# First attention layer: two-operand forms in place of copies and tensor_scalar on VectorE

## The reference

```
q, k, v = x @ Wq + bq, x @ Wk + bk, x @ Wv + bv          # 8 heads of 32
time_diff = edge_time - node_time[dst]
time_features = stack([sign(time_diff), log1p(abs(time_diff) / 3600)])
scores = sum(q[dst] * k[src]) * 32**-0.5 + time_features @ Wt + bt
alpha = softmax(scores, over all edges)                   # per head
out = segment_sum(alpha * v[src], dst) @ Wo + bo
```

## Time and profile before

| | us |
|---|---|
| median of three runs | 9245.88 |
| span of the profiled execution, first to last instruction | 9211.3 |
| first attention layer (loops of all engines) | about 1209 to 3996, 2787 |
| VectorE busy in that stretch | 1941.89 |
| GpSimd busy in that stretch | 1721.17 |
| TensorE busy in that stretch | 1501.30 |
| ScalarE busy in that stretch | 911.31 |

### The profile page before, as it was taken

One profiled execution on the slowest core, in us unless ns is written; L12 is line 12 of the kernel. 1 busy time (PEld: TensorE's weight loads), 2 busy tenths in 40 slices (PEclk: granted clock), 3 DMA queues, 4 the chain that ended last, 5 costly groups with the idle time before them and its releaser, 6 DMA issues. The chain is left out here.

```text
span 9211.3 us, 125505 instructions
## 1 busy us (share of the span) xinstructions
PE 5882.9 (64%) x27440; PEld 4000.9 (43%) x27441; DVE 5920.1 (64%) x16481; ACT 2399.3 (26%) x6580; POOL 5832.9 (63%) x6228
## 2 busy tenths in 40 slices
PE   2121145555555555559999996999999996545544
PEld 0010023333333333337777764566666664333333
DVE  4010056767777676658999986999999996222224
ACT  0000023333333333323333332444444442000000
POOL 5777756666666666647777762666666665666663
PEclk6555567777667767679999997999999998776776
DMA  1000033333333333323333352444444444333334
GB/s 67 1 8 10 10 88 90 91 90 89 92 88 92 87 88 87 90 57 84 88 90 87 85 83 55 120 126 123 126 123 126 123 125 95 90 91 91 90 90 53
DMA packets 406142, 779.80 MB, mean 85 GB/s; under 512 B 195939, under 2 KB 225357, under 8 KB 405197
## 3 DMA queue, kind: packets, MB, share of 16 engines
q0 software_dynamic: 279488, 712.60, 30.3%
q1 hardware_dynamic: 126348, 64.59, 2.5%
HBM read 736.75 MB, written 40.07 MB: 84 GB/s over the span
## 5 line engine op out<-in xcount | busy, mean ns | idle before, releaser
L982 POOL DMA_INDIRECT gat<-kv,rec_sb_d x896 | 861.6, 962 | 816.5 <-DVE big L1320 521.9
L1884 POOL DMA_INDIRECT gat<-y,rec_sb_s x892 | 1027.1, 1151 | 424.0 <-issue 285.4
L2153 POOL DMA_INDIRECT gat<-x,rec_sb_d x892 | 845.4, 948 | 477.7 <-issue 255.6
L1421 POOL DMA_INDIRECT gat<-kv,rec_sb_s x900 | 861.7, 957 | 415.2 <-issue 313.8
L2168 PE MATMUL ps<-gat,oh 128*128 128x256 f32 x1760 | 644.8, 535 | 676.2 <-DVE acc L2188 235.4
L1616 DVE TENSOR_REDUCE small<-ps 128x2 f32<-128x1024 f32 x884 | 1042.4, 1217 | 5.3 <-PE ps L1484 4.0
L434 POOL DMA_INDIRECT rec_d<-small x784 | 811.7, 1035 | 341.9 <-issue 263.2
L1925 PE MATMUL ps<-big,oh 128*128 128x256 f32 x3520 | 907.7, 390 | 0.0
L489 POOL DMA_INDIRECT rec_s<-wts,rows x770 | 758.7, 985 | 234.7 <-issue 234.7
L1028 PE MATMUL ps<-qz,work 128*128 x1792 | 770.2, 605 | 143.2 <-issue 125.7
L2168 PEld LDWEIGHTS ps<-gat,oh 128*128 128x128 f32 x1760 | 461.0, 273 | 859.7 <-issue 558.2
(11 more groups left out here) (278 smaller groups left out, 12710.2 us busy)
## 6 DMA issues: line engine op xcount, KB each, us to landing
gat<-kv,rec_sb_s POOLq DMA_INDIRECT x900
gat<-kv,rec_sb_d POOLq DMA_INDIRECT x896
rec_sb_s<-rec_s SPq DMA_DIRECT2D x448, 32.0 KB
gat<-y,rec_sb_s POOLq DMA_INDIRECT x892
gat<-x,rec_sb_d POOLq DMA_INDIRECT x892
rec_d<-small POOLq DMA_INDIRECT x784
rec_s<-wts,rows POOLq DMA_INDIRECT x770
rec_s<-gat SPq DMA_DIRECT2D x4, 1808.0 KB, 17.0
```

Source lines behind the costliest of these rows:

```text
L982: e.indirect_dma_start(out=gat[:, m.u, q, :], out_offset=None, in_=table, in_offset=bass.IndirectOffsetOnAxis(ap=r_sb[:, m.u, q, 0:1].bitc ...
L1421: e.indirect_dma_start(out=gat[:, m.u, q, :], out_offset=None, in_=table, in_offset=bass.IndirectOffsetOnAxis(ap=r_sb[:, m.u, q, 0:1].bitc ...
L1884: e.indirect_dma_start(out=rows_y[m.u][:, q, :], out_offset=None, in_=y1, in_offset=bass.IndirectOffsetOnAxis(ap=r_sb[:, m.u, q, 0:1].bitc ...
L2153: e.indirect_dma_start(out=gat[:, m.u, q, 0:D], out_offset=None, in_=x3, in_offset=bass.IndirectOffsetOnAxis(ap=r_sb[:, m.u, q, 0:1].bitca ...
```

## The change

Every VectorE instruction of the loop that had one tensor operand in SBUF as a copy or a `tensor_scalar` is written with two tensor operands in SBUF. A copy becomes `max(x, x)`. The one-hots become two instructions of 128 by 256 instead of four of 128 by 128, comparing two broadcast views; `oh` is given with the second. They stand where the first two stood; where the third and the fourth stood, nothing is left. The sign takes a column of -1 (`minus_one`) in place of the immediate.

```diff
+            minus_one = col(576, 4)
+            def two_one_hots(e, m, q):
+                if q == 0:
+                    have_record(e, m)
+                    e.wait_ge(s["sum"], m.done(U))
+                ins = V.tensor_tensor(oh[:, m.u, q:q + 2, :], bcast(iota[:, :], 1, [P, 2, P]),
+                                      bcast(r_sb[:, m.u, q:q + 2, 1], 2, [P, 2, P]), ALU.is_equal)
+                if q + 2 == Q:
+                    ins.then_inc(s["oh"], 1)
+
+            def move(to, of):
+                return V.tensor_tensor(to, of, of, ALU.max)
 # times_1
-                k = c(V.tensor_scalar(sg, td, 0.0, -1.0, ALU.is_gt, ALU.add))
+                k = c(V.scalar_tensor_tensor(sg, td, 0.0, minus_one, ALU.is_gt, ALU.add))
 # score_timed
                 k = c(V.transpose(mq32_t, mq32))
                 ja = bucket(e, a)
-                one_hot(e, nxt, 0)
+                two_one_hots(e, nxt, 0)
                 c.wait(k)
                 k = c(V.tensor_reduce(by_block[:, 0:1], mq32_t, AX.X, ALU.max))
-                one_hot(e, nxt, 1)
+                two_one_hots(e, nxt, 2)
                 c.wait(k)
                 for n in range(1, 4):
-                    k = c(V.tensor_copy(by_block[0:32, n:n + 1], by_block[32 * n:32 * n + 32, 0:1]))
-                one_hot(e, nxt, 2)
+                    k = c(move(by_block[0:32, n:n + 1], by_block[32 * n:32 * n + 32, 0:1]))
                 c.wait(k)
                 k = c(V.tensor_reduce(mr, by_block[0:32, :], AX.X, ALU.max))
-                one_hot(e, nxt, 3)
                 c.wait(k)
-                k = c(V.tensor_copy(top32[0:32, :], mr.to_broadcast([32, 32])))
+                k = c(move(top32[0:32, :], mr.to_broadcast([32, 32])))
...
                 for n in range(1, 4):
-                    k = c(V.tensor_copy(top32_t[32 * n:32 * n + 32, 0:H], top32_t[0:32, 0:H]))
+                    k = c(move(top32_t[32 * n:32 * n + 32, 0:H], top32_t[0:32, 0:H]))
...
-                V.tensor_scalar(mj, mn, 1.0, None, ALU.mult).then_inc(s["f"], 1)
+                move(mj, mn).then_inc(s["f"], 1)
```

More of the change, by code:

```diff
@@ L1338, in dve @@
                     c(V.memset(mq32, 0.0))
+                    c(V.memset(minus_one, -1.0))
                     c.wait()
@@ L1342, in dve @@
                 for m in range(AHEAD - 1):
+                    if timed:
+                        two_one_hots(e, Macro(0, m), 0)
+                        two_one_hots(e, Macro(0, m), 2)
+                        continue
                     for q in range(Q):
```

## The result

| | median us (runs) | lowest to highest |
|---|---|---|
| before | 9231.44 (7) | 9214.21 to 9260.86 |
| after | 9194.72 (7) | 9157.15 to 9222.61 |

The ratio is 0.995, with 0.993 to 0.9971 as its 95% interval: 37 us gained, where 84 were forecast. The profiled execution of after is the slowest of its seven (9222.61 us), so its span, 9.5 us longer than that of before, must not be read as a loss. It also shows that only 1.8 us lie around a span, not the 34.6 us of the forecast: that difference was the spread between runs.

A forecast was written before the change was run, and what follows sets the result against it. VectorE was taken to set the pace, with GpSimd 2.4 us per turn from doing so. 3 x 0.3 + 0.6 = 1.5 us per pass over 56 passes, 84 us, took 9246 to about 9160; range 8970 to 9300, for faster alone 9085 to 9225.

The forecast's parts named there:

- Faster, 9160: Whole kernel: median falls from 9246 to about 9160 us; faster was given 0.55, this forecast itself 0.38.
- The sum of 84 us: Changed layer: 0.3 us in each of three turns plus 0.6 in the long one, over 56 passes.
- The change can't touch the loop's jump: VectorE's loop: the 3.45 us ahead of L1313 once a pass of four turns would stay.
- Relief of the small forms, 0.3 us in each of three turns: VectorE's copies at L1258: two-operand forms stall less, saving 0.3 us in each of a pass's three calm turns.
- rival 2: VectorE's dependent instructions stall in GpSimd's burst whatever their form, so no change: 9246, less or more 40 us; chance 0.22.
- Calm turn unchanged: VectorE's turns other than the long one: shorter one-hots and unfilled gaps change them by -0.3 to +0.6 us, taken as 0.
- The stall of L1209 stays near 65 us: VectorE's L1209 keeps its form, so its idle time, 65.3 us in 168 turns, was to remain.
- A long turn gives back little, since ScalarE is late by itself: Once a pass, ScalarE's L1127 starts late without VectorE's doing, so the 15.29 us turn gives back only 0.6 us.
- Rival 3: GpSimd loses its rest, bringing a second long turn in some passes, 5.0 us each: slower, 9300 us; chance 0.18.
- GpSimd has 2.4 us per turn to spare: GpSimd waits 2.4 us per turn for L1320, so relief of VectorE can bring at most 537 us.
- Rival 1: The lock between VectorE's copies or tensor_scalars and GpSimd explains all: rewritten lines' stalls go, 312 us, 8970; chance 0.22.
- The signs named: Changed layer: 84 us shorter, one turn in four over 14 us, L1127 late, L1209 idle near 65 us; later stages unchanged.

The follow-up runs named there:

- experiment 1: Changed kernel with copies, sign and running maximum in their old forms, so only the one-hots are changed: 9196.24 us, 0.9947.
- experiment 2: Changed kernel with four tensor_scalar one-hots back at their old places, so only moves, sign and running maximum are changed: 9227.92 us, 0.9998.
- experiment 5: Kernel before and changed kernel, each with GpSimd's scatters of this layer left out: 8871.99 us (0.9619) and 8635.76 us (0.9355).
- experiment 4: Changed kernel with four two-operand one-hots of 128x128 at the old four places instead of two wide ones: 9160.87 us, 0.992.
- experiment 3: Changed kernel with three more semaphore increments per turn on VectorE, for which nobody waits: 9205.0 us, 0.9964.
- experiment 7: Changed kernel with GpSimd waiting, between gathers and scatters, until ScalarE has evacuated the transposes: 9000.29 us, 0.9763.
- k1: Kernel before, with scatters waiting for ScalarE's evacuation and the next turn's record copied ahead of them, on a third chip: 8456.67 us, 1.0035.
- k4: Kernel of experiment 1, with scatters waiting for ScalarE's evacuation and the next record copied ahead of them, on a third chip: 8483.6 us, 1.0067.
- k2: Changed kernel, with scatters waiting for ScalarE's evacuation and the next turn's record copied ahead of them, on a third chip: 8449.15 us, 1.0032.

## Why the prediction was right and wrong

- *Faster, 9160.* Measured 9194.72: the direction holds, and the time lies within the range. That is luck. The sum of 84 us was right in nothing but its order of size, for its terms were not what moved the time.
- *"The change can't touch the loop's jump."* This is the step that failed most. It removed nearly all of it: 149.5 to 19.1 us ahead of the multiply, 174 us over the layer. The row was in front of me, as was the row of queue 14 on the page, and I took 3.45 us once a pass for a property of jumps. A change that rewrites a loop must be asked what it does to the fetching of its code. That the one-hots' rewriting removed it, experiments 1, 2 and 5 show, and experiment 4 by its 169.2 us as well; that the count of instructions is the reason isn't shown, and experiment 3 speaks against it.
- *Relief of the small forms, 0.3 us in each of three turns.* Experiment 2 gives 0 (within 0.2% of the time). The stalls ahead of the moves stayed, as rival 2 said: 126.5 and 128.7 us for 121.1.
- *Calm turn unchanged.* It went from 9.68 to 9.27 us (1803.12 to 1812.39 in after), 0.1 us outside the bounds of -0.3 to +0.6.
- *The stall of L1209 stays near 65 us.* It fell to 21.8; those of L1244 and of the last move rose, from 16.8 to 36.4 and from 17.2 to 36.5. A stall falls on whatever VectorE has just then; its place is no property of the line. That was wrong, and with it the reasoning line by line from the earlier trace rows.
- *A long turn gives back little, since ScalarE is late by itself.* Right, and it is the core of the case. The long turns stayed, and grew by 0.5 us. ScalarE's release hangs on GpSimd's burst (experiments 5 and 7). But ScalarE is late by TensorE's signal and not by itself, and the earlier trace rows, which were to show the same wait elsewhere, are waits for TensorE's matmuls as far as k1's trace tells.
- *Rival 3, a second long turn.* Its mechanism came: 1.29 turns over 14 us per pass became 1.76. It comes with the jump's 3.45 us and not with the small forms: ScalarE starts over 5 us late in 40 to 47 of some 200 turns with the jump paid (before and experiment 4) and in 33 of 191 in experiment 2, but in 82 to 93 of some 193 without it (after, experiments 1 and 3). That the 3.45 us had served as GpSimd's rest once a pass is my reading; no run tests it. Its sum was too dark because some 174 us stood on the other side, not 84.
- *GpSimd has 2.4 us per turn to spare.* True as a mean, and misleading: in the pair read it waits 4.50 us for L1331 in one turn and not at all in the next, and the pair takes 24.96 us, as two mean turns of before do.
- *Rival 1, the lock alone, 8970.* Its 312 us are near only to the 236 us that the change brings without the scatters, and for another reason. With the scatters the stalls are there for two-operand forms as well.
- *The signs named.* One turn in four was to be over 14 us; it was 86 in 195. The sign of rival 2, the moves idling as the copies did, came. That of rival 3 came by half: more long turns, but GpSimd's wait ahead of the gathers fell, from 402.9 to 379.9 us. The stages behind the layer didn't keep their lengths, by the 23 us of the second layer.

The Trainium skill, page "SBUF — State Buffer", section "Who interferes with whom", which the prediction drew on, has ScalarE and TensorE wait for nobody. Here ScalarE starts over 5 us late 88 times in 196 with the scatters and never in 179 without. Since it waits for TensorE's signal, this is no evidence that SBUF's ports hold it up, and the traces neither bear the rule out nor refute it. What delays TensorE's signal and VectorE's steps until the burst ends isn't shown: only that it needs scatters in the loop, and that the form of VectorE's small instructions isn't the cause. Whether the third chip does it in the unaltered kernel is open.

## What to carry to other kernels

Before pricing stalls line by line, look at the idle time once per pass of the loop together with the queue of instruction fetches: where both come once a pass, the loop's code is being fetched again, and rewriting a few instructions can remove that (here 174 us of idle time), whatever their form is worth. Vary one thing at a time: here the fewer instructions and the new form came together, and experiment 4 shows that the new form of the one-hots moves the time by itself. Where two engines run in a ring with long bursts, a gain on one comes back as a wait unless the burst is given its place; one wait on the engine that isn't the bound (experiment 7) brought some 1.9% beside the change's own 0.5, on the chip where it ran. And run the kernels that are compared on one chip, and the unaltered one with them.

## What the runs showed of the hardware

- In each pass of the loop 5 packets of 8 KB went over the queue of instructions, two of them while VectorE stood still at the jump for 2.9 to 5.4 us (before; 3.4 to 3.8 in k1). With eight compute instructions fewer in a pass (280 recorded instead of 288) there were none; eight recorded semaphore increments more (288 again) didn't bring them back.
- In before and after, beside a burst of indirect DMAs on GpSimd, the semaphore behind TensorE's transposes changed up to 9.3 us (before: 7.7) after their start, where it otherwise takes under 1 us. In 54 of before's 64 turns in which it came over 1 us late, and in 87 of after's 96, this was 1.4 to 1.8 us behind the last indirect DMA. ScalarE started at once, 0.02 us behind it in the turn shown.
- The same kernel took 9241, 9221 and 8428 us on three chips. Of the 753 us between the spans of before and k1, 387 lie outside the changed layer.
- A copy of 32 x 8 lasted 203 (before), 223 (experiment 1) and 247 ns (k4) in the mean, the same move with two operands 158 to 161 (after, experiments 2 and 7, k2).
